# Feature stage of a four-stage network: projections as three single-pass products on high and low parts, in place of one fp32 product

## What is computed

```python
def _feature_map(t, K):
    f = jnp.einsum('hdf,bhld->bhlf', K, t)
    feats = jnp.concatenate([jax.nn.softmax(f, axis=-1), jax.nn.softmax(-f, axis=-1)], axis=-1)
    return jnp.maximum(feats, EPS)
q = _heads(x @ Wq); k = _heads(x @ Wk); v = _heads(x @ Wv)     # 16 heads of 64
qf = _feature_map(q, Kq); kf = _feature_map(k, Kk)
kv = jnp.cumsum(kf[:, :, :, None, :] * v[..., None], axis=2)
o = jnp.einsum('bhlf,bhldf->bhld', qf, kv)
z = jnp.einsum('bhlf,bhlf->bhl', qf, jnp.cumsum(kf, axis=2)) + EPS
o = o / z[..., None]
return o.transpose(0, 2, 1, 3).reshape(...) @ Wo
```

## Time and profile before

| | |
|---|---|
| median of 3 runs | 6131.73 us (6127.62 to 6131.87) |
| profiled execution | 6136.03 us, its span 6134.2 us |
| mean granted TensorE clock | 0.866 of 2.4 GHz |
| busy in the span | PE 4713.8 us (77%), DVE 4298.2 (70%), POOL 3353.0 (55%), ACT 2838.3 (46%) |
| feature stage | from about 470 to 1288 us; scores of the first head at 560.61 us |
| L672, the projection products | 192, from 497.1 us on; two records each, 592 ns the shortest, 1222 ns the longest record |
| L807, copies of the transposed input | 16, 383 ns each |

### The profile page before, as it was taken

One profiled execution on the slowest core, in us unless ns is written; L12 is line 12 of the kernel. 1 busy time (PEld: TensorE's weight loads), 2 busy tenths in 40 slices (PEclk: granted clock), 3 DMA queues, 4 the chain that ended last, 5 costly groups with the idle time before them and its releaser, 6 DMA issues. The chain is left out here.

```text
span 6134.2 us, 175865 instructions
## 1 busy us (share of the span) xinstructions
PE 4713.8 (77%) x70592; PEld 3658.9 (60%) x70592; DVE 4298.2 (70%) x6496; ACT 2838.3 (46%) x5349; POOL 3353.0 (55%) x1834
## 2 busy tenths in 40 slices
PE   4986999947887678885788866888668887678875
PEld 3664877745666456664566655666546665466664
DVE  4346999958886478873688836888358884588854
ACT  2552333315554355552455534555335554355542
POOL 0004666637775367762577725777347774367741
PEclk8897999968998789986899978999778997798887
DMA  1000000002222012220122211222102222022220
GB/s 29 0 0 19 1 0 0 0 32 57 54 54 65 4 45 54 54 62 20 38 57 56 56 28 31 54 54 54 41 18 54 54 54 55 7 52 53 54 60 22
DMA packets 151608, 229.83 MB, mean 37 GB/s; under 512 B 33038, under 2 KB 56460, under 8 KB 149900
## 3 DMA queue, kind: packets, MB, share of 16 engines
q1 hardware_dynamic: 150924, 219.36, 15.0%
HBM read 26.31 MB, written 4.19 MB: 5 GB/s over the span
## 5 line engine op out<-in xcount | busy, mean ns | idle before, releaser
L1993 POOL TENSOR_TENSOR spare<-raw,table 128x512 f32<-128x512 f32 x768 | 1318.7, 1743 | 296.5 <-ACT spare L1592 296.5
L2003 POOL TENSOR_TENSOR raw<-raw,rs 128x1024 f32<-128x1024 f32 x384 | 821.8, 2151 | 694.5 <-DVE rs L1782 694.5
L1761 DVE TENSOR_TENSOR raw<-raw,spare 128x1024 f32<-128x1024 f32 x384 | 795.8, 2072 | 13.2
L1754 DVE TENSOR_TENSOR raw<-raw,table 128x1024 f32<-128x1024 f32 x384 | 736.8, 1919 | 62.3 <-POOL spare L1993 57.8
L1400 PE MATMUL trn<-ident,E 128*128 128x128 f32 x1536 | 329.5, 353 | 475.2 <-POOL E L2031 353.7
L1804 DVE TENSOR_REDUCE mx<-sco 128x16 f32<-128x1024 f32 x192 | 235.1, 1225 | 533.9 <-PE sco L1385 533.8
L2031 POOL TENSOR_TENSOR E<-E,rden 128x1024 f32<-128x1024 f32 x192 | 447.3, 2330 | 258.2 <-DVE rden L1819 258.2
L1400 PEld LDWEIGHTS trn<-ident,E 128*128 128x128 f32 x1536 | 237.3, 182 | 550.2 <-issue 366.2
L1611 ACT ACTIVATE room<-trn 128x512 f32<-128x512 f32 x384 | 230.1, 599 | 580.5 <-PE trn L1400 580.1
L1366 PE MATMUL trn<-ident,raw 128*128 128x128 f32 x3072 | 484.7, 281 | 9.2 <-ACT kT L1600 3.8
L1748 DVE TENSOR_REDUCE ss<-spare 128x16 f32<-128x1024 f32 x384 | 464.1, 1209 | 16.5 <-ACT spare L1592 16.4
(11 more groups left out here) (220 smaller groups left out, 11388.7 us busy)
## 6 DMA issues: line engine op xcount, KB each, us to landing
Vw<-V SPq DMA_DIRECT2D x1344, 128.0 KB
Vw<-V SPq DMA_DIRECT2D x192, 64.0 KB
spare<-in_L_ffn_Wqkv SPq DMA_DIRECT2D x6, 1536.0 KB, 6.6
wo<-in_L_ffn_Wo SPq DMA_DIRECT2D x6, 512.0 KB, 3.9
X<-in_L_attn_x SPq DMA_DIRECT2D x16, 128.0 KB, 2.6
x_before_deep<-X SPq DMA_DIRECT2D x1, 2048.0 KB, 8.3
raw<-x_before_deep SPq DMA_DIRECT2D x1, 2048.0 KB, 8.0
out<-X SPq DMA_DIRECT2D x16, 128.0 KB, 2.0
```

Source lines behind the costliest of these rows:

```text
L1754: dve.tensor_tensor(x, x, table[:, part, 0, k][:, None, :].to_broadcast([P, H, HD]), ALU.mult).then_inc(cos_part, 1)
L1761: dve.tensor_tensor(x, x, t2[:, part], ALU.add).then_inc(summed, 1)
L1993: pool.tensor_tensor(dst[:, :, a], src[:, :, 1 - a], table[:, part, 1, k, 32 * a:32 * a + 32][:, None, :].to_broadcast([P, H, 32]), ALU.mu ...
L2003: pool.tensor_tensor(x, x, rs[:, at:at + H][:, :, None].to_broadcast([P, H, HD]), ALU.mult).then_inc(rotated, 1)
```

## The change

Both factors of the projections are held as a high part and a low part in float32r, a format whose product takes one pass. ScalarE writes the high parts (a copy that rounds), VectorE the low parts (the fp32 value less the high part), and each product becomes three that add up in the bank: high by low, low by high, high by high. The high parts are written where the plain copies were (the input) or ahead of them (the folded weights, whose copy was VectorE's and is now ScalarE's copy and then VectorE's subtraction). The value weights, before loaded in place, are loaded into `g_shifted` and split. To make room, the unfolded weights `g_wT` live in `g_oT`. Slot 0 now counts as drained when VectorE has written the low part of the input.

```diff
@@ feature_stage, TensorE: project @@
-                        t = pe.matmul(gen[:], xT[:, k * P:(k + 1) * P], wf[:, col:col + 512],
-                                      start=True, stop=True)
+                        x_hi, x_lo = xT_hi[:, k * P:(k + 1) * P], xT_lo[:, k * P:(k + 1) * P]
+                        pe.matmul(gen[:], x_hi, wf_lo[:, col:col + 512], start=True, stop=False)
+                        pe.matmul(gen[:], x_lo, wf_hi[:, col:col + 512], start=False, stop=False)
+                        t = pe.matmul(gen[:], x_hi, wf_hi[:, col:col + 512], start=False, stop=True)
...
-                    pe.wait_ge(fold_kept, count(j - 1))
+                    pe.wait_ge(fold_kept, count(j))
...
-            pe.wait_ge(fold_kept, count(4))
+            pe.wait_ge(fold_kept, count(5))
@@ ScalarE: project @@
-                        t = act.activation(xT[:], gen[:, 0:SEQ], ACT.Copy)
+                        act.activation(xT_hi[:], gen[:, 0:SEQ], ACT.Copy).then_inc(x_high, 1)
...
-                    t.then_inc(proj_drained, 1)
+                        t.then_inc(proj_drained, 1)
@@ ScalarE: start @@
+            act.wait_ge(loaded, LOADED)
+            act.activation(wf_hi[:, 2 * INNER:3 * INNER], wv, ACT.Copy).then_inc(fold_high, 1)
+            for j in range(4):
+                act.wait_ge(folded, count(j + 1))
+                part, a = divmod(j, 2)
+                to = wf_hi[:, part * INNER:(part + 1) * INNER].rearrange("p (r a f) -> p r a f", a=2, f=HD)
+                act.activation(to[:, :, a], sco[a][:].rearrange("p (r f) -> p r f", f=HD),
+                               ACT.Copy).then_inc(fold_high, 1)
+            act.wait_ge(fold_kept, count(1))
@@ VectorE: softmaxes @@
+                if step == F_PROJ_STEPS[0]:
+                    dve.wait_ge(x_high, count(n + 1))
+                    dve.tensor_tensor(xT_lo[:], gen[:, 0:SEQ], xT_hi[:].bitcast(F32),
+                                      ALU.subtract).then_inc(proj_drained, 1)
@@ VectorE: start @@
+            dve.wait_ge(fold_high, count(1))
+            dve.tensor_tensor(wf_lo[:, 2 * INNER:3 * INNER], wv, wf_hi[:, 2 * INNER:3 * INNER].bitcast(F32),
+                              ALU.subtract).then_inc(fold_kept, 1)
             for j in range(4):
-                dve.wait_ge(folded, count(j + 1))
+                dve.wait_ge(fold_high, count(j + 2))
                 part, a = divmod(j, 2)
-                to = wf[:, part * INNER:(part + 1) * INNER].rearrange("p (r a f) -> p r a f", a=2, f=HD)
-                dve.tensor_copy(to[:, :, a], sco[a][:].rearrange("p (r f) -> p r f", f=HD)).then_inc(fold_kept, 1)
+                hi_part = wf_hi[:, part * INNER:(part + 1) * INNER].rearrange("p (r a f) -> p r a f", a=2, f=HD)
+                lo_part = wf_lo[:, part * INNER:(part + 1) * INNER].rearrange("p (r a f) -> p r a f", a=2, f=HD)
+                dve.tensor_tensor(lo_part[:, :, a], sco[a][:].rearrange("p (r f) -> p r f", f=HD),
+                                  hi_part[:, :, a].bitcast(F32), ALU.subtract).then_inc(fold_kept, 1)
```

More of the change, by code:

```diff
@@ L586, in psum @@
             return ctx.enter_context(nc.psum_tensor(name, [P, n], F32))
-        wT = sb("g_wT", [P, 2, PAIRS, D])
         kern = sb("g_kern", [P, 2, PAIRS, HD])
-        wf = sb("g_wf", [P, 3 * INNER])
+        wf_hi = sb("g_wf_hi", [P, 3 * INNER], F32R)
+        wf_lo = sb("g_wf_lo", [P, 3 * INNER], F32R)
         wo = sb("g_wo", [P, PAIRS, D])
@@ L593, in feature_stage @@
         xs = sb("g_xs", [P, 2, D])
-        xT = sb("g_xT", [P, SEQ])
+        xT_hi = sb("g_xT_hi", [P, SEQ], F32R)
+        xT_lo = sb("g_xT_lo", [P, SEQ], F32R)
         raw = sb("g_raw", [P, 2, 2, INNER])
@@ L598, in feature_stage @@
         shifted = sb("g_shifted", [P, 2, H, 2, HD])
+        wv = shifted[:, 0].rearrange("p h s f -> p (h s f)")[:, 0:INNER]
         es = sb("g_es", [P, 2, H, 2])
@@ L608, in feature_stage @@
         oT = sb("g_oT", [P, PAIRS, SEQ])
+        wT = oT[:].rearrange("p r t -> p (r t)").rearrange("p (a r d) -> p a r d", a=2, d=D)
         sco = [psum("g_sco0"), psum("g_sco1")]
@@ L618, in feature_stage @@
         folded = sem("g_folded")
+        fold_high = sem("g_fold_high")
         fold_kept = sem("g_fold_kept")
+        x_high = sem("g_x_high")
         staged = sem("g_staged")
@@ L651, in _ @@
             sp.dma_start(kern[:, 1], w["Kk"].rearrange("(r h) d f -> (h d) r f", h=2)).then_inc(loaded, 16)
-            sp.dma_start(wf[:, 2 * INNER:3 * INNER], w["Wv"]).then_inc(loaded, 16)
+            sp.dma_start(wv, w["Wv"]).then_inc(loaded, 16)
             sp.dma_start(wo[:], w["Wo"].rearrange("(r p) n -> p r n", p=P)).then_inc(loaded, 16)
```

## The result

The changed kernel takes 6190.53 us (median of 6 runs, 6183.71 to 6210.06); the kernel before, beside it, 6130.87 us. The ratio is 1.0103 with a 95% interval of 1.0084 to 1.0121: slower by 1.0%, some 60 us, where 6124.8 us was forecast and 6104 to 6138 allowed. The profiled execution has a span of 6182.9 us and took 6184.71 us; before it was 6134.2 us.

What follows compares the result with a forecast made beforehand. TensorE sets the pace from head 0 to head 5, VectorE with GpSimd from there to head 0. -2.7 us (stage head) and -4.2 us (14 sequences) make -6.9 us: 6124.8 us from the median, range 6104 to 6138.

Steps and rivals of the forecast that it cites:

- the first sentence: Feature stage, about 470 to 1288 us of the 6134.2 us span: the change touches only this, nothing outside changes.
- A product on TensorE: Feature stage, each 512-column product: three passes take 0.70 us in place of 0.86, saving 0.16 us.
- The sign given for it: In the changed profile's loop, a product should take 0.70 us from its start to the next instruction.
- The subtraction: VectorE, ahead of head 5's mask: waits for ScalarE's input copy, making everything behind it 0.78 us later relative to TensorE.
- TensorE 0.64 us earlier at head 5: Heads 0 to 5 of a sequence: four products saving 0.16 us each bring TensorE to head 5 0.64 us earlier.
- VectorE's idle time of 0.44 us taken up behind head 5: VectorE's waits of 0.17 us at head 8 and 0.27 at head 12 vanish; a sequence gains about 0.3 us.
- Head of the stage: Stage start at half clock: 0.69 and 0.46 us added, 2.5 and 1.3 saved, so -2.7 us; between -1.4 and -2.7.
- The stage as a whole: Feature stage: -2.7 us at its head and -4.2 over 14 sequences make -6.9 us; chance 0.58.
- Rival A: Feature stage: TensorE's saving comes through, 31 us less, about 6102 us, or 6116 with half of it; chance 0.22.
- Rival B: Head 5: all 0.78 us of the subtraction's wait paid in each of 14 sequences, +9.5 us, 6141 us; chance 0.12.
- Rival C: Prologue: TensorE's clock may stay at 1.2 GHz for another stretch, 5.2 us over six products, 6130 us; chance 0.08.

Runs made afterwards that it cites:

- experiment 1: The changed kernel with 112 idle instructions in TensorE's program at the start of the deep stage: 6129.41 us, ratio 0.9997 to the kernel before.
- experiment 7: The changed kernel with one of the three passes alone and idle instructions putting the deep loops at places 41 and 174: 6113.38 us in one run.
- experiment 3: The changed kernel with 112 idle instructions and the low-part subtraction moved behind the feature copy of head 5: 6125.35 us, ratio 0.9985.

## Why the prediction was wrong

**The step that failed** is the first sentence: the stage runs from about 470 to 1288 us, "and nothing outside it changes". Nothing outside is rewritten, but TensorE's program is longer ahead of the deep stage's loops by 144 instructions. This put the loop of layers 0 to 4 from a place where the stop after the jump is covered (41) to one where it isn't (185), +61.7 us over five layers, some 2.5 us for each of 25 jumps (4.2 us before the masks in place of 3.7, and a second stop of about 2 us amid the scores); and the loop of the last layer from a bad place (174) to a good one (62), -8.6. Shown from both sides: the loss goes with 112 idle instructions in the changed kernel (0.9997) and comes with 144 in the kernel before (1.0118). It could have been doubted from the profile before: its last layer took 77.9 us for two sequences where the same lines in the layers ahead took 75.2.

**Point by point.**
- A product on TensorE, 0.16 us saved: right (1.08 to 0.92 us with the scores ahead). The sign given for it, 0.70 us from its start to the next instruction, reads 0.78, since the product starts 0.08 us earlier over the scores.
- The subtraction, 0.05 us of handover and 0.33 in the queue, everything behind 0.78 us later: right (0.03, 0.34, 0.78).
- TensorE 0.64 us earlier at head 5: right; from the start of head 0 to the input copy it is 16.81 us (836.28 to 853.09), before 17.47 (839.25 to 856.72), 0.66 less.
- VectorE's idle time of 0.44 us taken up behind head 5: 0.32 of it was. From the copy to head 0 it is 29.38 us (806.90 to 836.28), before 28.92 (810.33 to 839.25), 0.46 more where 0.78 - 0.44 = 0.34 was said. So a sequence gains 0.20 and not 0.30, and thirteen of them 2.8 us.
- Head of the stage -2.7 us: the third input copy, behind the head, is at 575.75 in place of 578.07, -2.3 with the 0.8 that was there before the stage; some -1.5 of its own, at the end of the range that takes nothing from the three later products.
- The stage as a whole, -6.9 us: -5.1 by the last input copy, -4.3 of its own. In experiment 1, with the deep loops where they were, this is a ratio of 0.9997 (0.9988 to 1.0006): the "same within 0.2%" that was forecast.
- Rival A (TensorE's saving comes through): refuted by experiment 7, where a further saving three times as large brings 0.44 us. Its 42.9 us counted every idle moment of VectorE as one that could be used; of the 50.9 us only 37.1 are waits on another engine, the rest are gaps between its own instructions, which stay.
- Rival B (the wait at head 5): its place was right, it costs 0.44 us a sequence (experiment 3), and the gain over heads 0 to 4 paid for it.
- Rival C (the clock): the granted clock is 1.00 from 570 us on in both kernels.

Not among the rivals: that the length of a program may be a cost of its own.

**Still open.** Why the kernel before at places 185 and 62 is 18 us slower than the changed one at the same places, and what makes the stop before the masks 3.8 us at one jump and 4.8 at another from one and the same place. That the stops are waits for instructions is the reading of the place rule and of the page; no trace here shows the fetch itself.

## What to carry to other kernels

Where an engine's program loops over more instructions than it holds (seen here for one loop of TensorE), a change that lengthens the program anywhere ahead moves the loop, and the jump back may cost more or less: here 12 idle instructions were worth 84 us, more than ten times what the change itself earned. Before judging an edit, compare the time of untouched loops in both profiles, and look for waits on "issue" some microseconds long at the start of a round; if they differ, bring the loop back to its place with idle instructions and measure again. And an instruction that waits for a handover belongs behind the work on its queue that doesn't need it: moving one subtraction by two places brought 0.44 us a sequence, more than the change's net 0.20.

## What the runs showed of the hardware

- A jump back of a TensorE loop of 2655 instructions stops it for 3.2 to 4.8 us, in the traces that have the first record behind it. The Trainium skill, "Runtime: NRT & Kernel Launch", section "Instruction fetch mechanics", says that such a branch stalls for a fetch; the number is from the rows here.
- A second stop follows, at a fixed instruction, as if the block after the target's were missing too: place + 2n is 203 or 204 for nine places from 73 to 201. It ends 2.8 to 3.8 us after the restart wherever it begins (1777.52 to 1780.87 from place 185, 1779.58 to 1783.10 from 123, 1786.96 to 1790.10 from 105).
- A 128x128 by 512 pass in float32r takes 0.23 us in a row (802.47, 802.70, 802.93) at 2.4 GHz; three of them 0.78 us behind scores, of which 0.08 overlap these.
- 123 idle instructions on TensorE between two layers cost 8.7 us from maximum to maximum, and TensorE idles 10 us longer there: 0.07 to 0.08 us each. 112 ahead of the deep stage, where TensorE waits for a normalisation, cost nothing visible: from the last input copy to the first row maximum it is 228.9 us with them and 228.6 without.
